# First self attention of a two-layer decoder: heads in pairs replaced by heads in quads

## The reference

```python
q = (X @ W_Q + b_Q).reshape(Bv, Tv, H_TOT, DH).transpose(0, 2, 1, 3)      # H_TOT = 64, DH = 16
k_base = (X @ W_K + b_K) ...                                              # 16 heads
v_base = (X @ W_V + b_V) ...
k = jnp.tile(k_base, (1, N_BR, 1, 1)); v = jnp.tile(v_base, (1, N_BR, 1, 1))
q, k = (_rope(q), _rope(k))
scores = jnp.einsum('bhtd,bhsd->bhts', q, k) * ATTNSCALE
key_self = jnp.clip(jnp.sum(k * k, axis=-1), 1e-06, None)
w = jax.nn.softplus(scores / jnp.sqrt(key_self)[:, :, None, :])
w = jnp.where(causal, w, 0.0)
w = w * jax.nn.sigmoid(SCALE * w)
w = jnp.where(w < sinks, 0.0, w)
total = jnp.sum(w, axis=-1, keepdims=True) + sinks + 1e-06
out = jnp.einsum('bhts,bhsd->bhtd', w / total, v) + (sinks / total) * v_null
y = jnp.einsum('bntc,ncd->bntd', context, W_O) + W_O_bias
return y.mean(axis=1)
```

## Time and profile before

| what | value |
|---|---|
| runs | 3092.99, 3099.23, 3093.82 us; median 3093.82 us |
| profiled execution | 3088.96 us, its span 3087.2 us |
| mean granted PE clock over the span | 0.928 |
| softplus of the changed stage | first at 52.9 us, last at 880.5 us of the span |
| last matmul of the changed stage's sums | 905.7 us |
| from batch to batch in the stage | 109.2 us |

### The profile page before, as it was taken

One profiled execution on the slowest core, in us unless ns is written; L12 is line 12 of the kernel. 1 busy time (PEld: TensorE's weight loads), 2 busy tenths in 40 slices (PEclk: granted clock), 3 DMA queues, 4 the chain that ended last, 5 costly groups with the idle time before them and its releaser, 6 DMA issues. The chain is left out here.

```text
span 3087.2 us, 46929 instructions
## 1 busy us (share of the span) xinstructions
PE 2711.5 (88%) x17384; PEld 2026.2 (66%) x17384; DVE 1762.0 (57%) x4040; ACT 1559.8 (51%) x3054; POOL 788.5 (26%) x887
## 2 busy tenths in 40 slices
PE   6889888988867689999979999999979999949998
PEld 3444444544436467776758888888867777748887
DVE  3555545544547566556546666666666565555454
ACT  2665656565645344444435555555555556542221
POOL 1122222212210144444531111111005566610000
PEclk8888988987979799999989999999989999979999
DMA  3000000000002211111010000000010000020000
GB/s 104 4 4 4 1 4 4 4 1 4 1 1 66 77 25 25 30 44 25 22 34 13 6 6 6 3 1 1 1 67 8 6 7 5 1 96 6 6 8 31
DMA packets 88753, 58.80 MB, mean 19 GB/s; under 512 B 55120, under 2 KB 78544, under 8 KB 88016
## 3 DMA queue, kind: packets, MB, share of 16 engines
q1 hardware_dynamic: 88528, 55.80, 6.1%
HBM read 39.00 MB, written 8.39 MB: 15 GB/s over the span
## 5 line engine op out<-in xcount | busy, mean ns | idle before, releaser
L674 DVE SCALAR_TENSOR_TENSOR a_w<-a_w,a_sinks 128x384 f32<-128x384 f32 x512 | 324.2, 698 | 69.8 <-ACT a_w L502 69.8
L464 ACT ACTIVATE a_w<-psum 128x1024 f32<-128x1024 f32 x192 | 190.7, 1026 | 299.4 <-PE psum L338 119.1
L1103 POOL TENSOR_SCALAR f_weights<-f_weights,f_sums 128x256 f32<-128x256 f32 x256 | 232.8, 927 | 271.3 <-DVE f_sums L1333 271.3
L2011 POOL TENSOR_SCALAR x_weights<-x_weights,x_sums 128x256 f32<-128x256 f32 x256 | 232.5, 927 | 271.4 <-DVE x_sums L2070 271.4
L1261 ACT ACTIVATE f_weights<-psum,f_negmax 128x256 f32<-128x256 f32 x256 | 118.0, 473 | 210.3 <-DVE f_negmax L1327 210.3
L1597 ACT ACTIVATE a_turned_w_hi<-psum 128x512 fp32r<-128x512 f32 x256 | 139.1, 595 | 151.7 <-PE psum L1507 151.7
L1981 ACT ACTIVATE x_weights<-x_masked_s,x_negmax 128x256 f32<-128x256 f32 x256 | 127.0, 497 | 136.2 <-DVE x_negmax L2062 136.2
L1713 DVE TENSOR_REDUCE a_negmax<-psum 128x1 f32<-128x1024 f32 x128 | 156.7, 1224 | 64.6 <-PE psum L119 60.5
L502 ACT ACTIVATE a_w<-a_w 128x1536 f32<-128x1536 f32 x128 | 179.4, 1472 | 0.4
L335 PE MATMUL psum<-a_qT,a_kT_half 32*128 32x512 f32 x512 | 160.3, 705 | 15.9 <-ACT a_w L464 13.9
L1675 POOL TENSOR_TENSOR a_xT_lo<-all_xnT_all,a_xT_hi 128x512 fp32r<-128x512 f32 x56 | 71.5, 1277 | 384.8 <-ACT a_xT_hi L1577 384.8
(11 more groups left out here) (359 smaller groups left out, 7464.1 us busy)
## 6 DMA issues: line engine op xcount, KB each, us to landing
f_xnT<-all_xnT_all SPq DMA_DIRECT2D x16, 256.0 KB, 2.4
f_pv_rows<-f_pv SPq DMA_DIRECT2D x8, 512.0 KB, 3.2
f_pv_groups<-f_pv_rows SPq DMA_DIRECT2D x8, 512.0 KB
f_w<-in_f_w SPq DMA_DIRECT2D x2, 2048.0 KB, 9.9
all_x_all<-in_x SPq DMA_DIRECT2D x1, 2048.0 KB, 8.6
a_xnT<-all_xnT_all SPq DMA_DIRECT2D x8, 256.0 KB, 2.3
x_xnT<-all_xnT_all SPq DMA_DIRECT2D x8, 256.0 KB, 2.3
x_ctxT<-in_x_ctxT SPq DMA_DIRECT2D x8, 256.0 KB, 2.9
```

The source lines that it names most:

```text
L464: act.activation(to, of, ACT.Softplus).then_inc(softened, 1)
L674: ins = dve.scalar_tensor_tensor(part, part, sinks[:, col:col + 1], part, ALU.is_ge, ALU.mult)
L1103: ins = pool.tensor_scalar(w, w, sums[:, k, h, t:t + 1], None, ALU.mult)
L2011: ins = pool.tensor_scalar(w, w, sums[:, k, h, t:t + 1], None, ALU.mult)
```

## The change

The unit becomes the quad. One score group is now four heads in the four strips of 32 rows, 4 score and 4 mask matmuls into four banks, softened by one activation over 128x2048. There are three groups to a quad, 12 to a batch instead of 24 slots. PSUM becomes two halves of four banks: groups 0 and 2 of quad m lie in half m, group 1 in half m+1 (mod 2), and all other work of step m goes into the half of quad m once its third group is softened. `beside_quad` gives the other work in two parts, FIRST before the sums of quad m-1 and LAST behind them. A quad's heads are now every other one of eight (`heads_of`), and `w` holds three quads instead of four pairs (two quads).

The swapped weights are gone. A projection item makes two chunks at once (4 matmuls into one bank), DVE swaps the halves by a shuffle of 128x512 into `swap`, and then as before two multiply instructions for each chunk, of which the second pair now reads `swap`. POOL adds two chunks in one instruction. The out projection is made in two halves of 8 matmuls. The values are projected from `xnT_all`; the DMAs to `xnT` and SP's block are gone, and so are the loads of `wqs` and `wks`. ACT's silus now follow directly on the third softplus of their own quad, and `take_sums` of quad m-1 stands behind the fourth silu of quad m (behind the second one for the third quad of a batch, where `take_turned` and Ln and Exp also stand).

```diff
-PAIRS_OF_HEADS, QUADS, SLOTS = NH // 2, NH // 4, 3
-PAIR_RING = 4
+QUADS, SLOTS = NH // 4, 3
+QUAD_RING = 3
...
+SWAP = [u // DH * DH + (u + DH // 2) % DH for u in range(32)]
...
+def heads_of(k):
+    return slice(8 * (k // 2) + k % 2, 8 * (k // 2) + 8, 2)
+def banks_of(m):
+    return m % 2 * 4
+def beside_quad(m):
+    b, k = divmod(m, QUADS)
+    if k == 0:
+        sent = [[("regroup", m - 2, 0, 0), ("regroup", m - 2, 1, 1), ("q", b, 2, 2)], [("out", b - 2, 1, 1)]]
+    elif k == 1:
+        sent = [[("v", b, 0, 0), ("q", b, 3, 1), ("regroup", m - 2, 0, 2)], [("regroup", m - 2, 1, 1), ("k", b + 1, 0, 2)]]
+    elif k == 2:
+        sent = [[("turn", b - 1, 0, 0), ("turn", b - 1, 1, 1), ("norm", b + 1, 0, 2)],
+                [("turn", b - 1, 2, 1), ("turn", b - 1, 3, 2), ("regroup", m - 2, 0, 3), ("regroup", m - 2, 1, 0),
+                 ("q", b + 1, 0, 1)]]
+    else:
+        sent = [[("regroup", m - 2, 0, 0), ("regroup", m - 2, 1, 1), ("q", b + 1, 1, 2)], [("out", b - 1, 0, 1)]]
+    made = lambda kind, of: 0 <= of < (ALL_QUADS if kind == "regroup" else B)
+    return [[(kind, of, i, banks_of(m) + bank) for kind, of, i, bank in part if made(kind, of)] for part in sent]
...
+SUM_BANKS = 3, 0
+SPAN = range(1 - QUADS, ALL_QUADS + QUADS + 1)
...
-        wq, wqs = s.sb("wq", [P, CC, BR * D]), s.sb("wqs", [P, CC, BR * D])
-        wk, wks, wv = s.sb("wk", [P, CC, D]), s.sb("wks", [P, CC, D]), s.sb("wv", [P, CC, D])
+        wq = s.sb("wq", [P, CC, BR * D])
+        wk, wv = s.sb("wk", [P, CC, D]), s.sb("wv", [P, CC, D])
         wo = s.sb("wo", [P, BR * CC, D])
...
-        xnT = s.sb("xnT", [P, CC, T])
...
+        swap = s.sb("swap", [P, 2, 2 * T])
...
-        w = s.sb("w", [P, PAIR_RING, 2, BR, COLS])
...
+        w = s.sb("w", [P, QUAD_RING, 4, BR, COLS])
...
-        @block.sync
-        def _(sp):
-            for b in range(B):
-
-                sp.wait_ge(v_done, b)
-                sp.dma_start(xnT[:], xnT_all[:, bass.ds(b, 1), :, :]).then_inc(v_x_here, 16)
...
+            def scores(m, group):
+                b, k = divmod(m, QUADS)
+                g, base = k // 2, banks_of(m + group % 2)
+                if group == 0 and k % 2 == 0:
+                    pe.wait_ge(kheads_ready, b * 2 + g + 1)
+                if group < 2 and k % 2 == 0:
+                    pe.wait_ge(rotated, TURNED_AT["q", b, 2 * g + group] + 1)
+                claim(range(base, base + 4), lambda bank: (softened, m * SLOTS + group + 1))
+                rows = [slice(32 * j, 32 * j + 32) for j in range(4)]
+                for j in range(4):
+                    keys, at = (slice(0, P), qT[rows[j], g, 2 * group:2 * group + 2, :]) if group < 2 else \
+                        (slice(P, T), qT[rows[j], g, :, P:T])
+                    pe.matmul(psum[:, base + j, :], kT_half[rows[j], k % 2, g, keys], at, start=True, stop=False)
+                for j in range(4):
+                    by_branch = psum[:, base + j, :].rearrange("p (r t) -> p r t", r=2 if group < 2 else BR)[:, :, 0:P]
+                    ins = pe.matmul(by_branch, ident_r[:], future[:].unsqueeze(1).to_broadcast([P, by_branch.shape[1], P]),
+                                    start=False, stop=True)
...
+                spare = psum[:, bank, :]
+                if kind in "qk":
+                    n = TURNED_AT[kind, of, i]
+                    claim([bank], lambda _: (proj_taken, n + 1))
+                    for z in range(2):
+                        weights, lo = (wk, z * P) if kind == "k" else (wq, (2 * (2 * (i % 2) + z) + i // 2) * P)
+                        for c in range(CC):
+                            ins = pe.matmul(spare[:, z * T:(z + 1) * T], weights[:, c, lo:lo + P], xnT_all[:, of, c, :],
...
+            for m in SPAN:
+                here, before = 0 <= m < ALL_QUADS, 0 <= m - 1 < ALL_QUADS
+                first, last = beside_quad(m)
+                if here:
+                    scores(m, 1)
+                    scores(m, 2)
+                if 0 <= m < ALL_QUADS - 1:
+                    scores(m + 1, 0)
+                for item in first:
+                    send(*item)
+                if before:
+                    for half in range(2):
+                        sum_half(m - 1, half)
+                for item in last:
+                    send(*item)
+                if m == -1:
+                    scores(0, 0)
...
+            def soften(m, group):
+                if group == 0:
+                    wait(act, summed, 2 * (m - QUAD_RING) + 2)
+                act.wait_ge(scored, m * GROUPS_OF_SCORES + group + 1)
+                wu = w[:, m % QUAD_RING]
+                bank = banks_of(m + group % 2)
+                of = psum[:, bank:bank + 4, :]
+                if group < 2:
+                    to, of = wu[:, :, 2 * group:2 * group + 2, 0:T], of.rearrange("p j (r t) -> p j r t", r=2)
                 else:
+                    to, of = (z.rearrange("p j r t -> p (j r) t") for z in (
+                        wu[:, :, :, T:COLS], of.rearrange("p j (r t) -> p j r t", r=BR)))
...
+            for m in SPAN:
+                here, before = 0 <= m < ALL_QUADS, 0 <= m - 1 < ALL_QUADS
+                turns = [item for part in beside_quad(m) for item in part if item[0] == "turn"]
+                if here:
                     for x in range(SLOTS):
+                        soften(m, x)
+                if here:
+                    act.preload_act_table_set("silu_and_others")
+                    act.wait_ge(softened, m * SLOTS + SLOTS)
+                for j in range(4):
+                    if here:
+                        wj = w[:, m % QUAD_RING, j].rearrange("p r t -> p (r t)")
+                        act.activation(wj, wj, ACT.Silu, scale=SILU_SCALE).then_inc(silu_done, 1)
+                    if j == 0:
+                        for _, b, i, bank in turns[:2]:
+                            take_turned(b, i, bank)
+                    if before and j == (1 if m % QUADS == 2 else 3):
+                        for half in range(2):
+                            take_sums(m - 1, half)
+                    if j == 1:
+                        for _, b, i, bank in turns[2:]:
+                            take_turned(b, i, bank)
+                ahead = m // QUADS + 1
+                if m % QUADS == 2 and ahead < B:
+                    act.preload_act_table_set("natural_log_exp_and_others")
+                    act.wait_ge(norm_taken, ahead + 1)
+                    act.activation(ksq[:], ksq[:], ACT.Ln).then_inc(ln_k, 1)
+                    act.wait_ge(ln_k, ahead + 1)
+                    act.activation(ksq[:], ksq[:], ACT.Exp, scale=-0.5, bias=ln_quarter[:, 0:1]).then_inc(knorm_ready, 1)
+                if here or m % QUADS == 2 and ahead < B:
+                    act.preload_act_table_set("softplus")
...
+                    n = TURNED_AT[kind, of, i]
+                    bias, cols = (bk, (0, 1)) if kind == "k" else (bq, [2 * (2 * (i % 2) + z) + i // 2 for z in range(2)])
+                    dve.wait_ge(projected, n + 1)
+                    dve.stream_shuffle(swap[:, n % 2, :], spare, SWAP).then_inc(swapped, 1)
+                    wait(dve, rotated, n - 1)
+                    for z in range(2):
+                        part = slice(z * T, (z + 1) * T)
+                        ins = dve.scalar_tensor_tensor(rot[n % 2][:, 0, part], spare[:, part], bias[:, 0, cols[z]:cols[z] + 1],
+                                                       rope[:, 0, :], ALU.add, ALU.mult)
+                    ins.then_inc(proj_taken, 1)
+                    dve.wait_ge(swapped, n + 1)
+                    for z in range(2):
+                        part = slice(z * T, (z + 1) * T)
+                        ins = dve.scalar_tensor_tensor(rot[n % 2][:, 1, part], swap[:, n % 2, part], bias[:, 1, cols[z]:cols[z] + 1],
+                                                       rope[:, 1, :], ALU.add, ALU.mult)
...
+            for m in SPAN:
+                here = 0 <= m < ALL_QUADS
+                first, last = ([item for item in part if item[0] != "turn"] for part in beside_quad(m))
+                for item in first:
+                    take(*item)
+                for j in range(2):
+                    if here:
+                        threshold(m, j)
+                for item in last:
+                    take(*item)
+                for j in range(2, 4):
+                    if here:
+                        threshold(m, j)
```

More of the change, by code:

```diff
@@ L232 @@
-REGROUPS = 8
-ROTATED = 2 + 2 * BR
-def rotations(b, kind, i, when):
-    place = i if when == HERE else 4 + i if kind == "k" else 6 + i
-    return b * ROTATED + 6 + place
-def quad_at(b, at, new, old):
-    if at >= 0:
-        return (at, b * QUADS + at) if new else None
-    return (QUADS + at, b * QUADS + at) if old else None
+ALL_QUADS = B * QUADS
+SWAP = [u // DH * DH + (u + DH // 2) % DH for u in range(32)]
+FIRST, LAST = range(2)
+GROUPS_OF_SCORES = 3
+def heads_of(k):
```

(43 more changed lines are left out.)

402 lines of the change are left out of this document (118 added, 284 removed).

## The result

After: 2871.43 us (median of 4 runs, 2870.45 to 2875.28); before, on the same chip, 3093.4. The ratio is 0.9281, interval 0.9265 to 0.9297. The forecast was 2840 in a range of 2770 to 2960, so 222 us were saved where 254 were forecast.

What follows compares the result with a forecast made beforehand. The first stage's batch, 109.2 us of PE work, low clock and holes, would become a 69 us ring of waits plus 9 us of low clock: 78. Eight batches save 249.6, loads 4, giving 2840 us, range 2770 to 2960.

Steps and rivals of the forecast that it cites:

- the ring: First stage: PE, ACT and DVE, with 62, 63 and 60 us of work, wait for each other; this sets the batch.
- (b): Rival, score groups: four strips of rows do not overlap beyond two; 95 us a batch, 2976 us; chance 0.08.
- (d): Rival, first stage: holes between PE's bursts keep its clock at 0.50; 124 us a batch, 3210 us; chance 0.05.
- (a): Rival, first stage: the ring runs as walked without loss by the clock; 69 us a batch, 2770 us; chance 0.15.
- the clock: PE in the first stage: low clock after holes costs 9 us a batch, bounds 0 and 20; before, 12.2.
- (e): Rival, first stage: the change only moves the bound; a batch stays near 109 us by waits; chance 0.03.
- The case of the sum: First stage: the forecast's own case, batches of 73 to 86 us, 2800 to 2905 us in all; chance 0.55.
- DVE takes the items of FIRST by 7: Path to group 1: DVE is through with FIRST 7 us after the quad's second softplus starts, then thresholds two heads.
- The walk: First stage, followed quad by quad from second softplus to second softplus: 15.5 + 17.2 + 20.3 + 15.5, rounded up 69 us a batch.
- Softplus still waits more than 20 us a batch: ACT in the first stage, above all quad 1 for DVE: a sign that the prediction is wrong; before, about 40 us.
- rival (c): First stage: more waits than found, from DVE's item order, bank claims and POOL; 92 us a batch, 2952 us; chance 0.14.
- PE's 62.1 us: PE's work per batch at full clock: 83.6 less 8.8 for the swapped projections and 12.7 for the scores.

Runs made afterwards that it cites:

- e5: Changed kernel with DVE taking LAST after one head and useless matmuls (2, 6, 10, 2 per quad) in PE's holes: 2799.77 us, ratio 0.9046.
- e1: Changed kernel with DVE taking the items of LAST after the threshold of one head, not two: 2826.35 us, ratio 0.9135.
- e2: Changed kernel with PE's holes filled by useless matmuls (5, 10, 10, 5 per quad) ahead of group 1: 2830.47 us, ratio 0.9152.
- e9: Changed kernel without the shuffle, PE making each q and k chunk twice to restore the second projection's cost: 2867.01 us, ratio 0.9263.
- e4: Changed kernel with each group's scores in two blocks of two strips, each with its masks, as before: 3174.58 us, ratio 1.0261.
- e7: Changed kernel with scores in two blocks of two strips and PE's holes filled by useless matmuls (5, 10, 10, 5): 2974.56 us, ratio 0.9604.
- e11: Changed kernel with POOL's sum of the rotary products for q and k cut from 512 to 32 columns: 2840.36 us, ratio 0.9179.
- e10: On e5, DVE takes a regroup's totals and reciprocals after all items of LAST: 2799.4 us, ratio 0.9047.

## Why the prediction was right, and where it was off

**Right.** PE's score work was what ACT waited for, and the ring, not an engine, is the bound after. The sums of ACT (63.6 for 63.4) and POOL, softplus, four strips in 1.07 us, the load (3.7 for 4 us) and the shuffle (0.74 for 0.69) held. Rivals (b) and (d) are excluded by the row at 221.18 and by a clock of 0.89; (a)'s 69 us a batch is nearly reached only where DVE's order and the clock are both mended (e5), and (e) is excluded by the batch of 82.1. The case of the sum came: 82.1 us is in its 73 to 86.

**The step that failed: "DVE takes the items of FIRST by 7".** It was 10.6 in quad 0 and 10.5 in quad 1. The walk counted group 0 of the next quad (1.8 us) in PE's total but not in the path to DVE, where it and the value projection stand ahead of the q chunk; DVE could begin on the chunk's bank at 7.9. The prediction's own costs give that time: 2.38 + 1.92 + 1.8 + 1.76 = 7.9 us, and DVE's shuffle, four products and a copy come behind it. From there: thresholds of two heads 5.3 instead of 5.1 (6.4 in quad 0, where POOL adds rotation and bias), items of LAST 2.5 instead of 3.2, group 1 on PE 3.2 at half clock instead of 1.9. Quad 1's softplus came at 21.7 instead of 17.2, and quads 0 and 3, forecast as "hidden by ACT's 15.5", waited 3 us each. "Softplus still waits more than 20 us a batch" was named as the sign of an error; it was 17 to 18, against some 4 in the walk. e1 shows the place by taking one head off this path: 45 us.

**The clock was mis-sized, in the other direction.** Forecast 9 us a batch; e2 gives 82.1 - 76.1 = 6.0. Low stretches were some 17 us a batch (from a mean clock of 0.90 over 82 us) for the 20 to 30 forecast (30.6 in the earlier trace rows). Walk 69, clock 6.0, and 7.1 that remain for order and thresholds: that is the 82.1, where the forecast had 69 and 9. The 7.1 were absent, and rival (c) describes their kind but not their size. That the forecast missed a batch by 4 us and not by 7 is luck: 3 us too much for the clock stood against them.

**Terms that were right in sum but not in place.** PE's 62.1 us were made from 8.8 for the second projection and 12.7 for the scores. The first bought nothing measurable (e9). The second, taken back, costs 303 us, by the estimate above some 88 for the work and the rest for the clock (e4, e7). The forecast had both as work of the same worth; on this ring, work in a hole was free, and work between a claim and a softplus cost nearly its length, and more where the clock fell with it. The 62.1 us themselves were some 3.6 too many: a group is 1.74 us for 1.92, one with long masks 2.21 for 2.38, and eight transposes take 0.9 for 1.2. PE is not what bounds the stage, so this did not show in the time. DVE's 4.1 us above the forecast are thresholds, 343.8 / 8 = 43.0 us a batch for 41.2, the shuffles' 0.2, and some 2 us of smaller operations that were not followed. e11 shows what POOL's rotation costs the thresholds: 343.8 - 306.2 = 37.6 us of the stage.

**The rule on PSUM.** The prediction had ACT's 69 us as the floor that is left when PE's work shrinks. (By the PSUM Bottleneck of the Trainium skill, "TensorEngine Tiling (Array Packing)", that could be the reading of PSUM. No run here shows this as the bound.) In the kernel as it was changed, DVE's order and the clock came first. In e5, with little else in the way, ACT is busy 63.9 and DVE 63.3 of 71.1 us, and the twelve softplus that read the scores are 22.4 us of ACT's.

**Open.** Why the clock fell in e7 at 340.8 us and not behind the same instructions a batch before; what two strips cost at full clock without useless matmuls; and what is left in e5 (56.2 us of waits before softplus in the stage), which e10 shows to be partly its own useless matmuls.

## What to carry to other kernels

When one engine stands between two producers, walk its queue item by item, with everything that its suppliers have queued ahead: one head's thresholds ahead of the copy that frees a bank cost 45 us, while an exchange of 70 us of PE work for 30 us of shuffles cost nothing either way. Price work by where it stands: here it was free in a hole of PE, or even repaid by the clock, and the same microseconds between freeing a bank and refilling it were paid nearly in full. And after a change that packs an engine better, look at the order of the others before looking for more packing: e1's few moved lines gave a fifth of what the whole change gave.

## What the hardware showed that was not expected

- **Narrow scores did not bring the clock back.** After a hole of 5.04 us two-strip scores ran at 0.50 for 17 us with no idle time (e4); after a hole of 5.05 us four-strip scores were at full clock after 6.5 us. The only edit is how many heads run side by side. Nor did two-strip scores always hold it: with the holes filled they ran two batches at 1.00, and from the next on the clock fell in their midst in every batch (0.91), each time behind no more idle time than 0.74 us (e7).
- **Useless matmuls made the kernel 41 us faster** (e2), and a two-strip kernel 200 us (e4 to e7).
- **POOL beside DVE.** Eight thresholds take 4.31 us alone, 5.33 beside one rotation of 128x512, 6.36 beside a rotation and the bias of 128x512 (1.39 + 1.58 us). With a rotation of 128x32 they take 4.31 again (e11, quad 1, beside 0.71 us), and with that and the bias 5.33 (quad 0). So each POOL instruction of 128x512 cost them 1.02 us of its own 1.4 to 1.7. (The Trainium skill, "SBUF — State Buffer", in "SBUF: two separate sides", has the port that both share as a lock held for the whole instruction when DVE has two inputs in SBUF; the trace agrees in kind, but shows less than the full length lost.)
